# Batches of value products and the ticks of the sums products in a fused attention kernel

## The reference

```python
mod = (_silu(L0_c) @ L0_wmod).reshape(L0_c.shape[0], 6, 1, -1)
h = _layernorm(x, axis=-1) * (1 + ca) + sa
q, k, v = h @ Wq, h @ Wk, h @ Wv              # then RoPE on q and k
att = jnp.einsum('bhgqd,bhkd->bhgqk', qg, k) / math.sqrt(D_HEAD)
att = jnp.where(causal[None, None, None], att, -jnp.inf)
probs = jax.nn.softmax(att, axis=-1)
ctx = jnp.einsum('bhgqk,bhkd->bhgqd', probs, v)
x = x + ga * (ctx @ Wo)
x = x + gb * _L0_ffn_ref(_layernorm(x) * (1 + cb) + sb, ...)
```

## Time and profile before

| | before |
|---|---|
| median of 3 runs | 2511.86 us (2506.41 to 2514.66) |
| span of the profiled execution | 2510.1 us |
| attention within it, about | 626 to 1737 us |
| PE busy | 97% of the span |
| DVE, POOL, ACT busy | 68%, 66%, 42% |

### The profile page before, as it was taken

The page is one execution under the profiler, slowest core; times in us unless marked ns, Lnnn a source line. Parts: engine busy times, 40 slices in busy tenths (PEclk is TensorE's granted clock), DMA queues, the critical chain, the costliest instruction groups (busy, mean ns, idle before and its releaser), DMA issues. The chain is left out here.

```text
span 2510.1 us, 36950 instructions
## 1 busy us (share of the span) xinstructions
PE 2433.2 (97%) x13716; PEld 1678.6 (67%) x13716; DVE 1698.5 (68%) x2878; ACT 1046.8 (42%) x1873; POOL 1650.9 (66%) x865
## 2 busy tenths in 40 slices
PE   5999999999999999999999999998999999999998
PEld 3788888887555555555555555554688788888886
DVE  4766666677888887888878888873655354455553
ACT  3433333331666666666666666665211111111111
POOL 3743333341798998999989999993755455555543
PEclk9999999999999999999999999999999999999999
DMA  6532333351535325344233334312433333333330
GB/s 229 201 118 85 115 113 116 122 155 72 161 99 145 73 66 160 82 114 108 66 89 82 82 94 137 82 48 93 134 97 96 100 94 101 110 93 100 110 93 25
DMA packets 179727, 267.49 MB, mean 107 GB/s; under 512 B 20508, under 2 KB 113884, under 8 KB 178400
## 3 DMA queue, kind: packets, MB, share of 16 engines
q1 hardware_dynamic: 179552, 265.13, 36.0%
HBM read 183.22 MB, written 80.81 MB: 105 GB/s over the span
## 5 line engine op out<-in xcount | busy, mean ns | idle before, releaser
L1072 POOL TENSOR_TENSOR p_sum<-p_sum,p_ring 128x1024 f32<-128x1024 f32 (+2 forms) x465 | 991.4, 2159 | 81.0 <-PE ctx_ps L1133 59.7
L263 DVE TENSOR_REDUCE neg_max<-scores_q 128x1 f32<-128x512 f32 (+1 forms) x1168 | 708.7, 655 | 124.0 <-PE scores_q L250 66.0
L966 ACT ACTIVATE p_ring<-scores 128x512 f32<-128x512 f32 (+1 forms) x896 | 453.0, 565 | 243.1 <-DVE scores L1020 178.6
L250 PE MATMUL scores_q<-k_stack,q_stack 96*128 96x512 f32 (+1 forms) x1473 | 442.6, 380 | 3.0 <-DVE neg_max L263 2.0
L1112 PE MATMUL scores<-q_stack,k_stack 98*128 98x512 f32 (+1 forms) x1216 | 423.6, 425 | 12.3 <-ACT p_ring L966 8.8
L617 POOL TENSOR_TENSOR roped_hilo<-roped_hilo 128x512 fp32r<-128x512 f32 x80 | 105.8, 1322 | 339.7 <-ACT roped_hilo L459 339.7
L1112 PEld LDWEIGHTS scores<-q_stack,k_stack 98*128 98x128 f32 x1216 | 198.4, 192 | 175.4 <-ACT p_ring L966 93.2
L250 PEld LDWEIGHTS scores_q<-k_stack,q_stack 96*128 96x128 f32 x1473 | 266.2, 192 | 71.2 <-DVE neg_max L263 36.3
L666 PE MATMUL proj_ps<-h_hi,w_hi 128*128 128x512 f32 x752 | 300.3, 399 | 0.7 <-POOL w_lo L606 0.7
L666 PE MATMUL proj_ps<-h_hi,w_lo 128*128 128x512 f32 x752 | 294.3, 391 | 0.0
L666 PE MATMUL proj_ps<-h_lo,w_hi 128*128 128x512 f32 x752 | 293.6, 390 | 0.0
(11 more groups left out here) (178 smaller groups left out, 3709.9 us busy)
## 6 DMA issues: line engine op xcount, KB each, us to landing
q_stack<-qk_t SPq DMA_DIRECT2D x96, 512.0 KB, 6.9
qk_t<-roped_hilo SPq DMA_DIRECT2D x80, 512.0 KB, 2.8
x_in<-in_L_attn_resid SPq DMA_DIRECT2D x32, 512.0 KB, 6.3
ctx_t<-ctx_raw SPq DMA_DIRECT2D x64, 256.0 KB, 5.6
prefetched<-in_L_wmod SPq DMA_DIRECT2D x4, 4096.0 KB, 13.3
prefetched<-ctx_t SPq DMA_DIRECT2D x31, 512.0 KB, 4.1
prefetched<-inv_t SPq DMA_DIRECT2D x124, 128.0 KB, 5.5
k_stack<-qk_t SPq DMA_DIRECT2D x96, 128.0 KB, 8.8
```

What stands on the lines that cost most here:

```text
L250: last = nc.tensor.matmul(dst[:, a, :], qs[0:MHI, h, i * P:(i + 1) * P], ks[0:MHI, lo:lo + w], start=not first and (a == 0 or not diag), s ...
L263: nc.vector.tensor_reduce(sh.negm[:, lo // HALF, hs[0]:hs[-1] + 1, i:i + 1], src, AX.X, ALU.max, negate=True).then_inc(sh.s_mx.sem, 1)
L966: nc.scalar.activation(p[:, a * per:(a + 1) * per, :], src[:, a * per:(a + 1) * per, :], ACT.Exp, scale=SM_SCALE).then_inc(s_ex.sem, 1)
L1072: nc.gpsimd.tensor_tensor(a, a, probs(n, u), ALU.add).then_inc(s_ap.sem, 1)
```

## The change

The value products go out in four batches a group, quads 0 to 3 at tick 7, 4 and 5 at tick 11, 6 and 7 at tick 15, 8 to 11 at tick 1 of the next group. The sums products of half 1 move from tick 9 to tick 7, those of half 0 from tick 16 to tick 15, so both stand directly ahead of a batch of values in PE's order. The last group's own sums ticks stay (6 and 12). No instruction is added or taken away, and the order of POOL's adds is the same.

```diff
 RING = 12
-BATCH = 2
+BATCHES = [(0, 1, 2, 3), (4, 5), (6, 7), (8, 9, 10, 11)]
+BATCH_ENDING = {b[-1]: b for b in BATCHES}
 QS = 3
 SS, MS = 2, 3
 LAG = 2
-SUM_AT = {1: 9, 0: 16}
+SUM_AT = {1: 7, 0: 15}
 SUM_AT_LAST = {1: 6, 0: 12}
@@ group_steps
         at, v = (n, u - LAG) if u >= LAG else (n - 1, u - LAG + NE)
-        if 0 <= at < NG and v == QUADS[QUAD_OF[v]][-1] and QUAD_OF[v] % BATCH == BATCH - 1:
-            steps += [("values", at, q) for q in range(QUAD_OF[v] - BATCH + 1, QUAD_OF[v] + 1)]
+        if 0 <= at < NG and v == QUADS[QUAD_OF[v]][-1]:
+            steps += [("values", at, q) for q in BATCH_ENDING.get(QUAD_OF[v], ())]
     return steps
```

## The result

| | before | changed |
|---|---|---|
| median | 2509.14 us (2503.84 to 2514.66, 4 runs) | 2631.15 us (2627.46 to 2640.29, 4 runs) |
| ratio | 1 | 1.05, 95% interval 1.0476 to 1.0525 |
| span of the profiled execution | 2510.1 us | 2638.5 us |
| mean period of a group | 34.42 us | 38.67 us |
| granted clock of PE, mean | 0.99 | 0.96 |

The change costs 122 us, where the forecast had 69 and its range ended at 2605. All of it lies in the attention loop: thirty periods of 38.67 - 34.42 = 4.25 us more are 127.5 us, and the spans differ by 128.4.

A forecast was written before the change was run, and what follows sets the result against it. PE was taken to set the 33.89 us period; -0.4, -0.05, +1.54 and +1.3 made it 36.3. Thirty periods by 2.36, with end corrections, gave +69 and 2580 us, range 2540 to 2605.

The forecast's parts named there:

- the two losses of the order: Attention loop on PE: uncovered value products at tick 1, +1.54 us, and DVE limiting ticks 2 to 7, +1.3 us.
- The sum: Attention loop: thirty periods by 2.36 us, +70.8, with corrections -5, +1 and +2.4, together +69, giving 2580 us.
- rival 3: PE waits at tick 0 and before tick 7 lower its clock, 1 us more a group: 2610 us; chance 0.10.
- Ticks 7 to 9, -0.4: PE in ticks 7 to 9: three runs of 3.65 us merge into 3.45, and edges save 0.2 more.
- The 0.3 us a run: PE's switches into and out of value or sums runs: each run removed saves 0.3 us, 1.2 for four.
- Tick 16 to tick 0, -0.05: PE there gets 0.93 us shorter, waiting for the maxima's row DMAs; sums cost 0.88 again at tick 15.
- Tick 1, +1.54: Quads 8 and 9 move to tick 1, where nothing hides their 1.64 us, less 0.10.
- Ticks 2 to 7, +1.3: Without a run at tick 5 DVE limits PE: 8.13 us from tick 2's scores to tick 7's sums; bounds 0 and 2.
- the -5: Four groups with a modulation product, 3.7 us of PE at tick 3: DVE catches up there, 5 us less.
- POOL's loop, 35.0: POOL's last add, tick 7's sums, quad 0, next first add: a floor of 35.0 us a group, under PE's 36.3.
- What bounds the kernel before: Steady attention group: PE, busy 33.62 of 33.89 us, sets the period, with POOL 1.4 us behind.

The follow-up runs named there:

- Shorter reductions: Changed kernel with five filler matmuls at tick 0, DVE reducing half the columns: 2537.47 us; the kernel before with the same half columns: 2481.55 us.
- the run without falls: Changed kernel with extra overwritten matmuls in PE's waits, five at tick 0, three at tick 6, one at tick 7: 2567.86 us.
- the fillers: Changed kernel with extra matmuls whose results are overwritten: five ahead of tick 0's scores, 2582.11 us; also three at tick 6 and one at tick 7, 2567.86 us.
- The last batch: Kernel before with only quads 8 to 11 merged at tick 1: 2575.05 us; the same with the maxima turned in tick 15: 2550.16 us.
- first batch only: Kernel before with only quads 0 to 3 merged at tick 7, sums still at ticks 9 and 16: 2554.21 us.

## Why the prediction was wrong

The direction and the two losses of the order were right, and the range was missed at its upper end by 26 us. The step that failed is PE's clock. The sum holds no term for it: it was put at nothing, and into rival 3 with a chance of 0.10 and a price of 1 us a group, on the argument that no new wait reaches 2.8 us. The runs show 2.08 us a group, 62 us.

- **Ticks 7 to 9, -0.4.** The run at tick 7 takes 3.37 us (3.45 forecast). From tick 8 to tick 16 it takes 13.54 (1071.72 to 1085.26), where the same work in the old runs would be 13.80, as above. Together 0.54 us less, so the saving is in the changed kernel and a little larger than forecast. It is no saving by itself: with the sums alone moved PE runs into banks that DVE still reads, and the period stays 33.90. The 0.3 us a run, read from starts of single products, was too much: two merges saved 0.4 there.
- **Tick 16 to tick 0, -0.05.** 1049.25 to 1055.64 is 6.39 us (6.5 forecast), the turn to the scores 4.06 (4.3 forecast, bounds 3.9 and 4.5). With the sums' 0.88 added again that is -0.16. Right, with the wait of 1.26 us where it was put.
- **Tick 1, +1.54.** 2.29 us from 1057.92 to 1060.21 against 0.79 in the earlier trace rows, 1.50. Right in size, half right in cause: the run at tick 19 covered the DMA, but it also gave DVE time. With the rows early there is still a loss (35.22 against 34.95), part of it at the early turn.
- **Ticks 2 to 7, +1.3.** 8.14 us against 8.13 forecast, with DVE busy without a gap from 1060.87 to 1069.40 and PE's wait for it ahead of the sums where it was put. Shorter reductions take 0.6 us off before POOL's loop stops them; that all of the 1.3 is DVE's reductions is not shown, as the masks and exponentials lie in the same chain and the longer wait, 0.61, is for ACT.
- **The sum.** 36.3 us forecast, 36.0 measured at full clock. The terms make 33.89 + 2.39 and the sum went on with 2.36, which is a slip of 1 us in all. The mean at full clock, from the run without falls, is 2.17 us a group above before, 65 us over the thirty periods against 70.8 - 5 forecast. That this fits so well is in part luck: a plain group costs 2.1 and not 2.36, and the -5 did not come, as the four groups with a modulation product take 8.0 us more, 2.0 each.
- **POOL's loop, 35.0.** 34.87 measured, gap 2.37 against 1.12 + 1.25 + 0.05 = 2.42. Right as a price, and right that it does not decide: in the changed kernel POOL idles 3.5 us in a full-clock group.
- **What bounds the kernel before.** I read PE, busy 33.62 of 33.89 us. Shorter reductions make that kernel 1.2 us a group faster, so DVE was on the path although it is idle for 5.9 us. Busy time of PE is not the same as PE unhindered. Its matmul row has one idle stretch above 0.15 us in that group, 0.24; the waits stand in the rows of its weight loads and of ACT, shown below the list: DVE's masks hold up ACT's exponentials, and these and DVE's reductions hold up PE's weight loads. I did not look there.
- **Rival 3.** I weighed the new waits against the one of 2.82 us in the earlier trace rows and argued that none reaches it. Waits of 1.26 us at tick 0, and 0.61, 0.18 and others in ticks 6 and 7, were enough. The price follows from what is lost in a low stretch: 37.5 against 36.0 is 1.5 us for one of 3.4 us, and 28 of the thirty periods have one or more, 154 us in all. The mean is 2.08 us a group, 62 us. I had taken 1 us, and left most of such a case out of the range.

The waits in one group of the kernel before (987 to 1021 us): who waited for whom, us in total, times, longest.

```profile
ACT p_ring L966 <- DVE scores L1020: 5.1, 7, 1.2
PEld scores L1112 <- ACT p_ring L966: 3.6, 5, 0.8
...
PEld scores_q L250 <- DVE neg_max L263: 1.2, 4, 0.4
```

That the waits are what lowers the clock is shown by the fillers: they add work and leave the full-clock period at 36.0, and with all three in place the granted clock is 1.00 over the whole loop. The last batch says it a second way, without filler: with the wait of 1.26 us 58.0 us are low, with the turn in tick 15 none. Open is which of the waits of ticks 6 and 7 matters, as both were filled together, how much of the 1.3 us of ticks 2 to 7 is DVE's reductions, and why the parts behind attention differ by 10 us between these profiles. No kernel here that computes the whole reference is faster than the one before.

## What to carry to other kernels

A run of long matmuls that nobody waits for may be the cover for a DMA and the time in which a slower engine catches up; before merging or moving such runs, lay the other engines' work of the stretch beside PE's and see who then sets the pace. A saving on PE of some tenths of a us at a switch is worth nothing where the next instruction waits for a bank. When a change puts waits of a microsecond, or several of half a one close together, into an otherwise dense stream of matmuls, price it a second time for the clock: here that nearly doubled the loss (62 us on top of 65).

## What the runs showed of the hardware

- One wait of 1.26 us on PE in each group of 35 us is enough for the granted clock to fall from 2.4 to 1.2 GHz in some groups and not in others of the same kernel: with the last batch alone, 16 of 30 periods held a low stretch and 14 did not. A group with one low stretch of 3.4 us behind tick 0 took 1.5 us more; where it came in ticks 5 to 7 (filler at tick 0, first batch only) it took 0.9 to 1.3 us more.
- The total of PE's idle time in a group did not decide it alone: 1.45 us with the one wait of 1.26 had falls, 1.28 us in four waits of at most 0.33 had none in thirty periods. Two waits of 0.24 and 0.61 us, with the first batch only, came with falls in 9 of 30 periods.
- Useless matmuls in such waits made the changed kernel faster by 49 us (five a group) and 63 us (nine a group) of 2631.
- Leaving and entering a run of 32-column products costs a tenth or three of a us in the starts, in line with the Trainium skill (TensorEngine Tiling (Array Packing), section Tiling Modes, Key Properties), which has a drain at each change of mode. Two runs fewer a group saved 0.4 us in their stretches, and none of it in the period, as PE then waited for other engines.
